# Attention by pairs of heads, with GpSimd taking the second head's products

## The reference

```python
x = x + moe0(groupnorm(x))            # 8 experts, top 2, and a shared expert
t = tokens(x)                         # 4 images x 256 tokens x 192
t = t + attention(layernorm(t))
t = t + moe1(layernorm(t))            # 16 experts, top 2, and a shared expert
```

```python
att = softmax(q @ k.T * D ** -0.5)    # 256 x 256 for each head and image
att = softmax(att * mask)             # mask: 0.5 where row % 64 == col % 64, else 1
out = (att @ v) @ w_out.T + b_out
```

## Time and profile before

| | us |
|---|---|
| runs | 543.4, 545.7, 549.63 |
| median | 545.7 |
| span of the profiled execution | 538.7 |

### The profile page before, as it was taken

One profiled execution on the slowest core, in us unless ns is written; L12 is line 12 of the kernel. 1 busy time (PEld: TensorE's weight loads), 2 busy tenths in 40 slices (PEclk: granted clock), 3 DMA queues, 4 the chain that ended last, 5 costly groups with the idle time before them and its releaser, 6 DMA issues.

```text
span 538.7 us, 7851 instructions
## 1 busy us (share of the span) xinstructions
PE 477.6 (89%) x2343; PEld 322.5 (60%) x2344; DVE 235.1 (44%) x676; ACT 162.4 (30%) x418; POOL 152.3 (28%) x135
## 2 busy tenths in 40 slices
PE   0999999999998169899999999889999999999990
PEld 0554766565656147766676666655767666666660
DVE  5157232222222344676666665638623333333330
ACT  2142002111112023466656565442012111121210
POOL 2000115556655100000000000000125565566652
PEclk9999699999999669899999999999899999999996
DMA  9992111222220593000000003764211221221100
GB/s 265 209 350 67 35 52 23 39 38 35 39 27 9 141 331 135 1 1 0 2 1 1 1 2 83 181 174 112 77 38 31 33 25 26 34 35 23 12 0 0
DMA packets 20956, 36.20 MB, mean 67 GB/s; under 512 B 6544, under 2 KB 17481, under 8 KB 20484
## 3 DMA queue, kind: packets, MB, share of 16 engines
q1 hardware_dynamic: 10468, 29.56, 19.3%
q0 software_dynamic: 10464, 6.33, 8.4%
HBM read 31.92 MB, written 8.45 MB: 75 GB/s over the span
## 4 chain that ended last, share of the span: by engine, by line
PE 69%; DMA 15%; DVE 6%; issue 5%; ACT 1%; POOL 1%; POOLq 1%; SPq 0%; DVEq 0%
PE bank L1158 15%; DMA sum<-y,slot_tok 12%; PE bank L1333 9%; PE bank L1097 8%; PE bank L1173 6%; PE bank L1320 6%; PE bank L1127 4%; PE bank L1275 4%; PE bank L1289 3%; PE bank L1165 2%; PE bank L1322 2%; PE bank L1368 2%; PE bank L1134 1%; PE bank L1079 1%; PE bank L1304 1%
## 5 line engine op out<-in xcount | busy, mean ns | idle before, releaser
L473 POOL DMA_INDIRECT rows<-xn_rows,slot_tok x56 | 58.4, 1042 | 131.5 <-DVEq L800 90.6
L1158 PE MATMUL bank<-w_first,rows_t 96*128 x248 | 85.4, 487 | 0.2 <-issue 0.2
L1173 PE MATMUL bank<-w_second,hid_t 128*128 x370 | 71.4, 333 | 8.3 <-issue 6.3
L859 DVE TENSOR_SCALAR y<-bank,slot_w 128x192 f32<-128x192 f32 x54 | 22.6, 418 | 102.5 <-PE bank L1173 83.6
L1173 PEld LDWEIGHTS bank<-w_second,hid_t 128*128 128x128 f32 x370 | 58.7, 190 | 13.5 <-issue 13.1
L484 POOL DMA_INDIRECT out<-y,slot_tok x31 | 48.9, 1577 | 47.4 <-DMA out<-y,slot_tok 28.2
L1158 PEld LDWEIGHTS bank<-w_first,rows_t 96*128 96x128 f32 x248 | 44.6, 190 | 25.5 <-issue 0.7
L631 ACT ACTIVATE scratch<-bank,neg_max 128x256 f32<-128x256 f32 x96 | 44.6, 470 | 39.2 <-DVE neg_max L948 34.4
L1333 PE MATMUL bank<-scratch,w_first 128*32 128x256 f32 x192 | 50.9, 390 | 0.0
L522 POOL COPY act_h<-o_inv 128x256 f32<-128x256 f32 x12 | 4.8, 400 | 162.7 <-DVE o_inv L979 162.0
L484 POOL DMA_INDIRECT sum<-y,slot_tok x23 | 36.3, 1577 | 36.3 <-DMA sum<-y,slot_tok 23.7
(11 more groups left out here) (172 smaller groups left out, 649.3 us busy)
## 6 DMA issues: line engine op xcount, KB each, us to landing
w_first<-in_gate_up SPq DMA_DIRECT2D x16, 576.0 KB
w_second<-in_down SPq DMA_DIRECT2D x1, 4608.0 KB, 24.5
w_first<-in_fc SPq DMA_DIRECT2D x1, 3072.0 KB
w_second<-in_fc SPq DMA_DIRECT2D x1, 3072.0 KB, 28.5
xn_rows<-xn_tok SPq DMA_DIRECT2D x2, 768.0 KB, 5.9
rows<-xn_rows,slot_tok POOLq DMA_INDIRECT x56, 2.7
w_first<-in_x_t SPq DMA_DIRECT2D x2, 384.0 KB, 4.4
w_first<-in_w SPq DMA_DIRECT2D x1, 768.0 KB, 7.0
```

Source lines behind the costliest of these rows:

```text
L473: pool.indirect_dma_start(rows[b % 2][:], None, xn_rows[L.l], bass.IndirectOffsetOnAxis(slot_tok[:, b:b + 1].bitcast(U32), 0), bounds_chec ...
L1158: ins = pe.matmul(bank[:, 5 + g, 0:I1], rows_t[0:CH, k, :], w(CH, (k * 2 + g) * I1, I1), start=(k == 0), stop=(k == NCH - 1))
L1173: ins = pe.matmul(bank[:, 1, 0:C], hid_t[:, tile(ic)], w(P, ic * C, C), start=(ic == 0), stop=(ic == L.IC - 1))
```

## The change

The attention now runs over 24 pairs of heads. Scores of a pair fill two whole banks, 2 * (p % 2) and the one behind. One `neg_maximum` reads both (1024 elements, four maxima). `exp_scores` does the four tiles of a pair. `attention` takes the reciprocal of four sums, signals `exp_inv_ready`, and does the products of the pair's first head, now in place in `e1`. GpSimd's `second_head` does the second head's: two multiplications by the inverse sums (128x256 each), a wait for both, and one multiplication by the mask (128x512). `att_transpose` does eight transposes, the identity matmuls being transposes too, four after VectorE's signal and four after GpSimd's, into banks 4 and 5. `exp_att` is one instruction over 128x1024. `weigh_values` is done once for four heads, with the heads inside the key tiles, so that consecutive matmuls go to different column groups. The sums of a chunk lie in bank 6 behind its outputs, the spread inverses always in bank 7. `p2_t` has three buffers of a pair's size, two of them in the room of tiles that are idle in this stage. SyncE waits for 24 signals of the scores.

```diff
-        e1 = [scratch_at(512 * i, 2, TOKENS_IMG) for i in range(3)]
-        att = [scratch_at(512 * (3 + i), 2, TOKENS_IMG) for i in range(2)]
+        e1 = [scratch_at(1024 * i, 4, TOKENS_IMG) for i in range(3)]
@@ GpSimd
+            def second_head(p):
+                pool.wait_ge(exp_inv_ready, p + 1)
+                for q in (2, 3):
+                    nc.gpsimd.tensor_scalar(e1[p % 3][:, q, :], e1[p % 3][:, q, :], exp_inv[:, p % 2, q:q + 1], None,
+                                            ALU.mult).then_inc(pool_half, 1)
+                pool.wait_ge(pool_half, 2 * (p + 1))
+                nc.gpsimd.tensor_tensor(e1[p % 3][:, 2:4, :], e1[p % 3][:, 2:4, :], bc(mask, 1, [P, 2, TOKENS_IMG]),
+                                        ALU.mult).then_inc(att2_ready, 1)
+            for p in range(N_PAIRS):
+                second_head(p)
+                if chunk_at(p, 2) is not None:
+                    widen(chunk_at(p, 2))
+            widen(N_CHUNKS - 1)
@@ ScalarE
+            exp_scores(0)
+            exp_scores(1)
+            for p in range(N_PAIRS):
+                if p + 2 < N_PAIRS:
+                    exp_scores(p + 2)
+                exp_att(p)
+                if chunk_at(p, 1) is not None:
+                    out_copy(chunk_at(p, 1))
+            out_copy(N_CHUNKS - 1)
@@ VectorE
+            def attention(p):
+                dve.wait_ge(e1_ready, p + 1)
+                if p >= 2:
+                    dve.wait_ge(att2_ready, p - 1)
+                go(v.reciprocal(exp_inv[:, p % 2, :], exp_sum[:, p % 4, :]))
+                dve.sem_inc(exp_inv_ready, 1)
+                for q in range(2):
+                    ins = v.scalar_tensor_tensor(e1[p % 3][:, q, :], e1[p % 3][:, q, :], exp_inv[:, p % 2, q:q + 1],
                                                  mask, ALU.mult, ALU.mult)
+            for p in range(N_PAIRS):
+                if p + 2 < N_PAIRS:
+                    neg_maximum(p + 2)
+                attention(p)
+                if chunk_at(p, 2) is not None:
+                    invert_sums(chunk_at(p, 2))
+                if chunk_at(p, 3) is not None:
+                    out_norm(chunk_at(p, 3))
+                if (chunk_at(p, 4) or 0) % HC == HC - 1:
+                    residual(chunk_at(p, 4) // HC)
+            ln_stats(0)
+            out_norm(N_CHUNKS - 2)
+            invert_sums(N_CHUNKS - 1)
+            ln_rows(2, 0)
+            out_norm(N_CHUNKS - 1)
+            residual(IMAGES - 1)
@@ TensorE
+            def scores(p):
+                if p >= 2:
+                    pe.wait_ge(e1_ready, p - 1)
+            def att_transpose(p):
+                for m in range(2):
+                    pe.wait_ge((att_ready, att2_ready)[m], p + 1)
+                    if p and m == 0:
+                        pe.wait_ge(p2_ready, p)
+                    for kt in range(2):
+                        for qt in range(2):
+                            ins = pe.transpose(bank[:, 4 + m, (kt * 2 + qt) * P:(kt * 2 + qt + 1) * P],
+                                               e1[p % 3][:, 2 * m + qt, tile(kt)], ident)
+                ins.then_inc(att_t_ps, 1)
+            def weigh_values(c):
+                pe.wait_ge(p2_ready, PAIRS_CHUNK * (c + 1))
                 for kt in range(2):
+                    for g in range(HPC):
+                        p = c * PAIRS_CHUNK + g // 2
+                        ins = pe.matmul(bank[g * HG:(g + 1) * HG, 6, 0:TOKENS_IMG],
+                                        v_tok[:, 2 * img + kt, (c % HC) * HPC + g, :], p2_t[p % 3][:, 2 * (g % 2) + kt, :],
+                                        start=(kt == 0), stop=(kt == 1))
+            for p in range(N_PAIRS):
+                if p + 2 < N_PAIRS:
+                    scores(p + 2)
+                att_transpose(p)
+                if chunk_at(p, 1) is not None:
+                    weigh_values(chunk_at(p, 1))
+                if chunk_at(p, 2) is not None:
+                    sums_by_token(chunk_at(p, 2))
+                if chunk_at(p, 3) is not None:
+                    spread_inverses(chunk_at(p, 3))
+                if (chunk_at(p, 4) or 0) % HC == HC - 1:
+                    project(chunk_at(p, 4) // HC)
```

More of the change, by code:

```diff
@@ L362, in build, with chunk_at @@
         N_HEADS = IMAGES * HEADS
[L363 to L378, removed]
+        N_PAIRS = N_HEADS // 2
+        N_CHUNKS = N_HEADS // HPC
+        PAIRS_CHUNK = HPC // 2
+        def chunk_at(p, lag):
+            c = (p - lag + 1) // PAIRS_CHUNK - 1
+            if c == N_CHUNKS - 1 or (p - lag + 1) % PAIRS_CHUNK or c < 0 or c >= N_CHUNKS:
+                return None
+            return c
+        SUMS_AT = TOKENS_IMG
         HALF = T // 2
@@ L516, in _, with widen @@
             pool_blocks(pool, L0, sum0)
-            for c in range(N_HEADS // HPC):
+            def widen(c):
                 pool.wait_ge(inv_ready, c + 1)
@@ L959, in _ @@
                               ).then_inc(v_out, 1)
[L961 to L969, removed]
+            def attention(p):
[6 more added lines that the diff above has]
+                    ins = v.scalar_tensor_tensor(e1[p % 3][:, q, :], e1[p % 3][:, q, :], exp_inv[:, p % 2, q:q + 1],
                                                  mask, ALU.mult, ALU.mult)
-                    if qt == 0:
+                    if q == 0:
                         step(ins)
@@ L1291, in scores @@
                                             start=(part is k_high), stop=(part is k_low))
-                            if qt == 1 and part is k_low:
-                                ins.then_inc(sc_ps, 1)
+                ins.then_inc(sc_ps, 1)
             pe.wait_ge(parts_ready, 2 * QKC)
             scores(0)
+            scores(1)
             for n in range(NT // 2):
@@ L1308, in _ @@
             pe.wait_ge(v_out, NT // 2)
[L1310 to L1313, removed]
-                for kt in range(2):
[L1315 to L1323, removed]
@@ L1340, in sums_by_token, with spread_inverses @@
                 pe.wait_ge(o_raw_ready, c + 1)
-                if sums_bank(c) == 0:
-                    pe.wait_ge(e1_ready, 2 * N_HEADS)
-                elif c and c % HC == 0:
+                for qt in range(2):
+                    o = SUMS_AT + qt * HPC
+                    ins = pe.matmul(bank[:, 6, o:o + HPC], o_raw[:, c % 2, tile(qt)], sum_row,
+                                    start=True, stop=True)
+                ins.then_inc(sums_ps, 1)
+            def spread_inverses(c):
+                pe.wait_ge(wide_ready, c + 1)
+                if c and c % HC == 0:
                     pe.wait_ge(x_new, c // HC)
@@ L1348, in sums_by_token @@
                 for qt in range(2):
-                    o = qt * HPC
-                    ins = pe.matmul(bank[:, sums_bank(c), o:o + HPC], o_raw[:, c % 2, tile(qt)], sum_row,
-                                    start=True, stop=True)
-                ins.then_inc(sums_ps, 1)
[L1354 to L1358, removed]
+                    ins = pe.transpose(bank[:, 7, tile(qt)], o_inv_wide[:, qt].rearrange("p g d -> p (g d)"), ident)
                 ins.then_inc(spread_ps, 1)
@@ L1370, in project @@
                 ins.then_inc(proj_ps, 1)
[L1374 to L1385, removed]
-                if (chunk_at(n, SUMS + 3) or 0) % HC == HC - 1:
-                    project(chunk_at(n, SUMS + 3) // HC)
-            pe.wait_ge(p2_ready, N_HEADS)
+            for p in range(N_PAIRS):
[10 more added lines that the diff above has]
+                    project(chunk_at(p, 4) // HC)
+            weigh_values(N_CHUNKS - 1)
+            spread_inverses(N_CHUNKS - 2)
+            sums_by_token(N_CHUNKS - 1)
+            spread_inverses(N_CHUNKS - 1)
+            project(IMAGES - 1)
             norm_transposes(2, 0)
```

87 lines of the change are left out of this document (39 added, 48 removed).

## The result

The changed kernel takes 645.9 us (median of 638.4 to 646.5) beside 547.7 us before: a ratio of 1.180 with a 95% interval of 1.171 to 1.189. Ratios leave out executions that are more than 1.5% above the fastest of the same kernel; medians don't. The profiled span is 643.6 us. From the first exponential of the scores to the start of the last projection the attention took 125.1 us (222.60 to 347.70) and takes 219.3 us (230.4 to 449.74).

What follows compares the result with a forecast made beforehand. TensorE alone bounded the old attention (123.8 us); after, waits closed through four queues: 103.2 us outside TensorE, 61.5 in it, 30.8 for lowered clock. Stage +71.7, tail +1.5: 545.7 + 73 = 619 us, range 575 to 665.

Steps and rivals of the forecast that it cites:

- The likeliest case: Whole kernel: closed waits through four queues plus a lowered TensorE clock, 619 us; chance 0.55.
- The ring: Attention: waits close through four queues within a step, so the period is the sum; 164.7 us against 123.8 at full clock.
- the signs that were named: Attention: chunk period 13 to 17 us, TensorE and VectorE idle waits, clock near 0.7, GpSimd busy about 55 us.
- The maximum: VectorE's maximum of a pair's scores, 1024 elements instead of 512: 1.14 us per pair.
- the term that was mis-sized: GpSimd's second head per pair: two scalings 0.8, wait 0.1, mask product 1.3, plus 0.45 for interference: 2.65 us.
- The allowance for the hold-up: GpSimd beside VectorE's products, standing in each other's way: 0 to 0.88 us per pair allowed, 0.45 taken.
- TensorE's part: Attention: TensorE's work between the waits, 28.8 + 24.1 + 8.6, together 61.5 us at full clock, 30.8 more when lowered.
- The lower level's share: Attention: half of TensorE's 61.5 us of work runs at half speed, taking 30.8 us more.
- The rival without overlap: Value matmuls: column groups don't overlap, 2.8 us more in each of 12 chunks, 669 us; chance 0.13.
- 1.5 us of tail: After the attention: ln_rows(2, 0) now stands before the last out_norm, +1.5 us.
- The 7.0 us: Whole kernel before: median 545.7 minus profiled span 538.7, taken as what lies around the span.
- The rival with the largest load as the period: Attention: queues find slack, largest load sets the period, 6.5 us a chunk, stage 78, time 501 us; chance 0.06.

Runs made afterwards that it cites:

- e_open: Changed kernel with VectorE taking attention(p) first, then its chunk parts one step later, then neg_maximum(p+2); GpSimd's widening copy one step later too: 532.7 us.
- e_order: Changed kernel with one call moved: VectorE takes attention(p) before neg_maximum(p+2): 592.3 us, ratio 1.087 to the kernel before.
- e_keep: Changed kernel with idle transposes on TensorE in its two waits of each pair (16 and 10), results unused: 607.1 us, ratio 1.119 to before.
- e_col: Changed kernel with a chunk's value matmuls looped with heads outside and key tiles inside: 646.8 us, ratio 1.180 to the kernel before.
- e_open_keep: e_open with eight idle transposes a pair on TensorE before it waits for VectorE's signal, results unused: 525.3 us, ratio 0.963 to the kernel before.

## Why the prediction was right, and what it had too small

Forecast 619 us, in a range of 575 to 665; measured 645.9. The likeliest case was the one that came.

- **The ring.** Shown: the chain has its links in the order given, and e_open, with the same work in another order, is 113 us faster. Of the signs that were named, the chunk's period (16.64 us, 13 to 17 forecast) and the idle times before the transposes and the maximum came; the clock fell further than forecast (0.60, near 0.7 forecast). My account of it was not complete: VectorE's parts for the chunk close the ring a second time, which I only saw in e_order.
- **The maximum** was put at 1.14 us: 309.60 to 310.74 is 1.14. From reciprocal to GpSimd 0.25 was forecast, 0.33 measured.
- **GpSimd** is the term that was mis-sized: 2.65 us forecast, 3.45 measured (301.60 to 305.05), and 85 us busy in the stage instead of about 55. The mask product was right (1.3 against 1.26). The scalings were put at the copy's 0.4 us and take 0.91 alone, more for an element than a product of two tensors (1.04 for 512). The allowance for the hold-up was 0.45, the row shows 0.28 on GpSimd. Outside TensorE the ring's step has 3.82 us (301.27 to 305.09) and 1.14, together 4.96; over 24 pairs that is 24 x (4.96 - 4.3) = 16 us more than forecast.
- **TensorE's part.** 219.3 - 24 x 4.96 = 100 us, 92 forecast. The lower level's share was right: e_keep, at 0.98, has 186.9 us where the changed kernel has 219.3, so it gives back 32, 30.8 forecast. By my estimate the other 6 are TensorE's work at full clock: 186.9 - 24 x 4.96 = 68 instead of 61.5. Which of its parts was too small stays open.
- **Value matmuls.** 1.1 us at full clock was taken; e_keep's sixteen instructions run from 301.69 to the spreading at 302.70, 1.01. The rival without overlap is out. By the Trainium skill (TensorEngine Tiling (Array Packing), "Tiling Modes") four column tiles run in parallel, and the trace agrees: four instructions start within 0.03 us.
- **Outside the stage.** I counted nothing but 1.5 us of tail. In the profiled runs the stage starts 7.8 us later and what follows is 2.9 us longer. The start differs by 12 us between the experiments (219.3 in e_open, 231.7 in e_col), for kernels that are alike up to there, so I don't read a cause into it. The 7.0 us that I took as lying around the span were misread: the run of the changed kernel that was profiled took 645.5 us, 1.9 more than its span, so the profiled execution of the kernel before took some 541. The forecast adds differences to the median, and so this does no harm to it.
- **The rival with the largest load as the period** failed as argued: no engine is busy for more than 54% of the stage. What it promised, 501, was not reached with the ring open either. That the largest load would set the period comes nearest in e_open_keep, where the load is GpSimd's: 3.7 to 4.0 us a pair, and not the 2.65 counted.

## What to carry to other kernels

Before work is moved to an idle engine, write down for one step what each queue waits for and what is queued behind the wait: if the way leads back to the start within the same step, the period is the sum of all links, and each hand-over makes it longer. In an in-order queue the call whose inputs are old goes first, and the one that waits for this step's end goes last. Here moving the maximum was worth 54 us, and moving the chunk's parts as well another 60, without one instruction more or less. And in this stage a TensorE that got gaps also got slower (0.99 before, 0.60 after), so that it paid twice. Once a ring is open, look again at the moved work: with the clock back, the engine that was to help was the one waited for.

## What the runs showed that I had not expected

- Value matmuls of different column groups start together even where the program issues one group's four instructions before the next group's (e_col: 307.59 and 307.62).
- GpSimd's multiplication by one number for each partition takes 0.91 us for 128x256, its product with a spread operand 1.04 us for twice as much.
- Idle transposes, 16 and 10 a pair, made the changed kernel 39 us faster, and eight a pair made e_open 7 us faster.
